# Weighted values summed over a batch's heads in two PSUM banks, batches unrolled

## The reference

```python
q, k, v = (einsum('btm,mhd->bthd', x, w) for w in (w_aq, w_ak, w_av))
q, k = _rope(q), _rope(k)
s = einsum('bihd,bjhd->bhij', q, k) / 128 - 1e30 * (i < j)
p = softmax(s, axis=-1)
o = einsum('bhij,bjhd->bihd', p, v)
r = einsum('bihd,hdm->bim', o, w_ao)        # summed over the heads
x = layernorm(x + r)
h = silu(tlin(x, w1_w, w1_s)) * tlin(x, w2_w, w2_s)
h = gelu(tlin(h, h1_w, h1_s)); h = gelu(tlin(h, h2_w, h2_s))   # erf form
return layernorm(x + tlin(h, w3_w, w3_s))
```

## Time and profile before

| | |
|---|---|
| median of three runs (lowest, highest) | 1098.11 us (1096.88, 1100.96) |
| span of the profiled execution | 1099.5 us |
| instructions | 20887 |
| PE busy, PE weight loads busy | 1008.7 us (92%), 837.4 us (76%) |
| DVE busy | 890.4 us (81%) |
| ACT busy | 657.7 us (60%) |
| POOL busy | 598.5 us (54%) |
| last matmul of attention | about 807.6 us |

### The profile page before, as it was taken

The page is one execution under the profiler, slowest core; times in us unless marked ns, Lnnn a source line. Parts: engine busy times, 40 slices in busy tenths (PEclk is TensorE's granted clock), DMA queues, the critical chain, the costliest instruction groups (busy, mean ns, idle before and its releaser), DMA issues. The chain is left out here.

```text
span 1099.5 us, 20887 instructions
## 1 busy us (share of the span) xinstructions
PE 1008.7 (92%) x5648; PEld 837.4 (76%) x5648; DVE 890.4 (81%) x1803; ACT 657.7 (60%) x1383; POOL 598.5 (54%) x536
## 2 busy tenths in 40 slices
PE   2699999999999999999999999999939999999995
PEld 1588787877878787887878788788727878788784
DVE  4888898989988899998889999898855758576744
ACT  4476776767776676777767777676625252252531
POOL 3667767777777778777777877777540100000000
PEclk8799999999999999999999999999978999999998
DMA  8542222732223242222223122222020000000000
GB/s 281 164 134 49 58 72 63 218 86 57 57 50 74 58 114 86 57 57 61 64 67 105 48 57 58 67 64 60 1 78 1 1 1 20 1 19 0 1 20 19
DMA packets 33838, 69.99 MB, mean 64 GB/s; under 512 B 5520, under 2 KB 7056, under 8 KB 32272
## 3 DMA queue, kind: packets, MB, share of 16 engines
q1 hardware_dynamic: 30976, 62.81, 21.4%
q10 hardware_dynamic: 2832, 6.82, 1.7%
HBM read 24.26 MB, written 7.34 MB: 29 GB/s over the span
## 5 line engine op out<-in xcount | busy, mean ns | idle before, releaser
L737 POOL TENSOR_SCALAR probs<-probs,inv_sum 128x128 f32<-128x128 f32 (+7 forms) x256 | 237.6, 928 | 178.5 <-DVE inv_sum L653 178.5
L554 ACT ACTIVATE pT<-psum 128x512 fp32r<-128x512 f32 (+3 forms) x384 | 176.7, 490 | 146.9 <-PE psum L420 144.7
L310 PE MATMUL psum<-pT,vals 128*128 128x512 f32 (+3 forms) x1152 | 246.9, 355 | 1.6 <-DVE rT L695 1.6
L542 ACT ACTIVATE probs<-psum,neg_max 128x128 f32<-128x128 f32 (+7 forms) x256 | 190.5, 744 | 52.5 <-DVE neg_max L647 49.0
L663 DVE TENSOR_TENSOR pT<-psum,pT 128x512 fp32r<-128x512 f32 (+3 forms) x384 | 199.8, 547 | 15.7 <-ACT pT L554 12.6
L310 PEld LDWEIGHTS psum<-pT,vals 128*128 128x128 f32 x1152 | 191.8, 193 | 24.1 <-DVE pT L663 1.7
L647 DVE TENSOR_REDUCE neg_max<-psum 128x1 f32<-128x128 f32 (+7 forms) x256 | 190.9, 746 | 11.0 <-PE psum L411 10.9
L420 PE MATMUL psum<-ident,probs 128*128 128x128 f32 x1152 | 178.5, 281 | 21.9 <-DVE pT L663 15.4
L742 POOL TENSOR_TENSOR swapped<-swapped,rope 128x512 f32<-128x512 f32 x128 | 165.4, 1292 | 40.5 <-DMA swapped<-proj 40.4
L749 POOL TENSOR_TENSOR qk<-swapped,qk 128x512 fp32r<-128x512 f32 x128 | 179.4, 1402 | 3.6 <-ACT qk L574 3.6
L918 PE MATMUL ps<-hid,w 128*128 128x512 f32 x768 | 181.3, 396 | 0.0
(11 more groups left out here) (78 smaller groups left out, 1241.7 us busy)
## 6 DMA issues: line engine op xcount, KB each, us to landing
swapped<-proj SPq DMA_DIRECT2D x256, 128.0 KB, 2.3
w_stage<-qk_split SPq DMA_DIRECT2D x30, 256.0 KB, 2.7
x_static<-x_moving SPq DMA_DIRECT2D x4, 1024.0 KB, 5.0
wv_stage<-v_split SPq DMA_DIRECT2D x15, 256.0 KB, 2.6
x_split<-ffn_raw ACTq DMA_DIRECT2D x2, 1024.0 KB, 5.9
ffn_raw<-g SPq DMA_DIRECT2D x2, 1024.0 KB, 8.0
x_moving<-x_split SPq DMA_DIRECT2D x2, 1024.0 KB, 4.9
out<-y SPq DMA_DIRECT2D x4, 512.0 KB, 2.6
```

The lines of the kernel that those rows point to most:

```text
L310: ins = nc.tensor.matmul(out_ap, left[a], right[b], start=first and i == 0, stop=last and i == 2)
L542: nc.scalar.activation(probs[:, ib % 4, :width].rearrange("p (h c) -> p h c", h=halves), score_ps[:, ib % 2, :halves, :half], ACT.Exp, bia ...
L554: nc.scalar.activation(pT[chunk][:, 0, 4 * f:4 * f + n_blocks, (ib % 4) * P:(ib % 4 + 1) * P], bank("t", head[1], nth)[:, :n_blocks * P].r ...
L737: nc.gpsimd.tensor_scalar(p, p, inv_sum[:, n:n + 1], 1.0, ALU.mult, ALU.mult).then_inc(probs_ready[0], 1)
```

## The change

The result of `attend` is no longer added head by head. The two halves of the tokens have a bank each (6 and 7), and the matmuls of all eight heads of a batch accumulate there; only the first matmul of the batch's first head overwrites. `take_batch` copies each half to `rT` once per batch, at the steps where the adds stood, and only the first head of the next batch waits for that. The zeroing of `rT` goes. Bank 6 leaves the set that fills, q and k tiles and value tiles share, so that banks 4 and 5 and the lent ones remain; the fourth value tile moves from step 6 to step 7. The loop over pairs 1 to 14 becomes, per batch, one pair written out and a loop over the other three (two in the last batch, whose last pair is written out), so that the batch is known wherever tokens are addressed: value tiles read `x_moving` directly and `x_static` with its four DMAs goes.

```diff
-V_STEP = (4, 5, 6, 6)
+V_STEP = (4, 5, 6, 7)
-ADD0_STEP, ADD1_STEP = 0, 4
+TAKE0_STEP, TAKE1_STEP = 0, 4
-PV_BANK = 7
+PV_BANK = 6
...
-                    uses[use] = [min([4, 5, 6] + lent, key=lambda b: last[b])]
+                    uses[use] = [min([4, 5] + lent, key=lambda b: last[b])]
...
-    pv_ps = psum[:, PV_BANK * BANK:]
+    pv_ps = psum[:, PV_BANK * BANK:].rearrange("p (k c) -> p k c", k=CHUNKS)
...
-            body((-1, 1), s)
-        steps(0, body)
-        with eng.Fori(1, PAIRS - 1) as pair:
-            steps(pair, body)
-        steps(PAIRS - 1, body)
+            body((-1, 1), s, 0)
+        for b in range(B):
+            steps(b, 0, body)
+            with eng.Fori(1, PAIRS_OF - (b == B - 1)) as hp:
+                steps(b, hp, body)
+        steps(B - 1, PAIRS_OF - 1, body)
...
             def stage_x_moving(b):
-                sp.wait_ge(qk_projected[0], NQK * H * (b - 1))
-                sp.wait_ge(x_fixed, 16 * b)
-                sp.dma_start(dst.bitcast(F32), src).then_inc(x_moved, 16)
+                wait_for_pair(sp, v_projected, PAIRS_OF * (b - 1) - 1, NV - 1)
+                sp.dma_start(x_moving[:, b % 2].bitcast(F32), x_split[b - 2]).then_inc(x_moved, 16)
...
-                    if not dynamic:
-                        sp.dma_start(x_static[:].bitcast(F32), x_half.bitcast(F32)).then_inc(x_fixed, 16)
...
-                                          [x_static[:, part, t0:t0 + P] for part in range(2)],
+                                          [x_moving[:, b % 2, part, t0:t0 + P] for part in range(2)],
...
-                    wait_for(pe, pv_added, *earlier(head, chunk, 1, CHUNKS))
+                    if in_batch(head) == 0:
+                        wait_for_pair(pe, pv_taken, number(head) // H - 1, chunk)
...
-                    last = split_products(pv_ps[:, i0:], [vals[:, part, jb, parity(head)] for part in range(2)],
+                    last = split_products(pv_ps[:, chunk, i0:], [vals[:, part, jb, parity(head)] for part in range(2)],
                                           [pT[chunk][:, part, jb, i0:] for part in range(2)],
-                                          jb == 0, jb == 4 * chunk + 3)
+                                          jb == 0 and in_batch(head) == 0,
+                                          jb == 4 * chunk + 3, in_batch(head) != 0)
...
-            def add_head(head, chunk):
+            def take_batch(head, chunk):
-                if not exists(head):
+                if in_batch(head) != H - 1 or not exists(head):
                     return
...
-                wait_for(dve, pv_added, *earlier(head, chunk, 2, CHUNKS))
-                nc.vector.tensor_tensor(acc, pv_ps[:], acc, ALU.add).then_inc(pv_added[0], 1)
+                nc.vector.tensor_copy(rT[:, col:col + BANK], pv_ps[:, chunk]).then_inc(pv_taken[0], 1)
...
-            nc.gpsimd.memset(rT[:], 0.0).then_inc(r_zero, 1)
```

More of the change, by code:

```diff
@@ L246, in run_pairs, with steps, in_batch @@
         for s in range(NI):
-            body((-1, 1), s)
-        steps(0, body)
-        with eng.Fori(1, PAIRS - 1) as pair:
-            steps(pair, body)
-        steps(PAIRS - 1, body)
+            body((-1, 1), s, 0)
[4 more added lines that the diff above has]
+        steps(B - 1, PAIRS_OF - 1, body)
         for s in range(NI):
-            body((PAIRS, 0), s)
-    def steps(pair, body):
+            body((PAIRS, 0), s, B)
+    def steps(b, hp, body):
         for off in range(2):
             for s in range(NI):
-                body((pair, off), s)
+                body((PAIRS_OF * b + hp, off), s, b)
+    def in_batch(head):
+        return number(head) % H if isinstance(head[0], int) else None
     def rope_tasks(head, s, steps):
@@ L304, in wait_for_banks, with split_products @@
                 break
-    def split_products(out_ap, left, right, first, last):
+    def split_products(out_ap, left, right, first, last, onto_earlier=False):
         terms = ((0, 0), (0, 1), (1, 0))
         for i, (a, b) in enumerate(terms):
-            ins = nc.tensor.matmul(out_ap, left[a], right[b], start=first and i == 0, stop=last and i == 2)
+            ins = nc.tensor.matmul(out_ap, left[a], right[b], start=first and i == 0, stop=last and i == 2,
+                                   skip_group_check=onto_earlier)
         return ins
@@ L373, in stage_pair @@
                         stage_for_values()
[L375 to L380, removed]
             stage_pair(0, 0)
             sp.wait_ge(w_saved, W_SAVED)
-            with sp.Fori(1, H // 2) as hp:
+            with sp.Fori(1, PAIRS_OF) as hp:
                 stage_pair(0, hp)
@@ L388, in _ @@
                 sp.dma_start(ffn_raw[:, base:base + src.shape[1]], src).then_inc(ffn_loaded, 16)
-            with sp.Fori(1, B - 1) as b:
-                stage_batch(b)
-            stage_batch(B - 1)
+            for b in range(1, B):
+                stage_pair(b, 0)
+                if b < B - 1:
+                    stage_x_moving(b + 1)
+                with sp.Fori(1, PAIRS_OF) as hp:
+                    stage_pair(b, hp)
         @block.tensor
@@ L490, in step @@
                 for c in v_tasks(head, s):
-                    project_v(head[0], c)
+                    project_v(head[0], b, c)
                 if s in PV0_PIECES and exists(head):
@@ L582, in values_high, with step @@
                                      bank("v", 0, nth), ACT.Copy).then_inc(v_high[0], 1)
-            def step(head, s):
+            def step(head, s, b):
                 ahead = step_on(head, (s + 1) // NI)
@@ L714, in step @@
                     negative_max(step_on(head, (s + 2) // NI), (s + 2) % NI)
-                if s == ADD0_STEP:
-                    add_head(step_on(head, -1), 0)
-                if s == ADD1_STEP:
-                    add_head(step_on(head, -1), 1)
+                if s == TAKE0_STEP:
+                    take_batch(step_on(head, -1), 0)
+                if s == TAKE1_STEP:
+                    take_batch(step_on(head, -1), 1)
                 if exists(head):
```

29 lines of the change are left out of this document (8 added, 21 removed).

## The result

The change makes the kernel slower: 1155.53 us (median of 4 runs, 1151.47 to 1161.36) against 1097.86 us (4 runs on the same chip), a ratio of 1.0525 with a 95% interval of 1.0493 to 1.0558. The prediction was 1169 us, in a range of 1124 to 1194. The profiled execution has a span of 1155.5 us, against 1099.5; a span runs from the first instruction to the last, and the device time of that same execution was 1157.39 us.

What follows compares the result with a forecast made beforehand. PE was taken to bound attention. The profiled 1099.5 us, plus 56 for bank waits, plus 17 for the clock, minus 1.6 at attention's end, gave 1170.9; less 1.4 to the runs' median, rounded to 1169 us, range 1124 to 1194.

Steps and rivals of the forecast that it cites:

- Mechanism and a pair's price: Value tiles wait for banks released by DVE's subtraction of a fill; +3.5 us a pair (2.0 to 4.5), +56 us over 16.
- the bound with DVE free: At v0, were DVE free, copy and subtraction of 4a would still leave a wait of 1.45 us.
- Off 1 unchanged: In off 1 an earlier subtraction gains nothing, since the scores behind it wait for POOL's low part; taken as 0.
- waits of off 1 absorb the stalls: Rival: engines catch up while PE stands in off 0, off 1's 1.5 us go, no clock cost; 1128 us, 15%.
- The path of off 1 gets longer: Rival: v3's later copy makes ACT, then POOL, 0.8 us late in off 1; 13 us on top, 1182 us, 10%.
- Faster: Rival: subtractions run ahead of PE, no bank is late, PE regains 1.8 us a pair and the clock; 1057 us, 6%.
- no change: Rival: banks late in name only, adds were hidden, only 1.6 us at the end of attention seen; 1096 us, 4%.
- Unrolling and token copies at 0: Ends of loop turns and token copies cost PE nothing, so 14 turns becoming 11 and dropping the copies gain 0.
- The clock: PE waits of 2.2 us at v0 were to bring half clock in 13 of 16 pairs; +17 us (0 to +27).
- 10 more at 1.7 us: Clock term: ten additional stretches of half clock on PE, each costing 1.7 us; +17 us.
- some 15: Sign that the forecast is right: some 15 stretches of half clock on PE.
- The end of attention: PE's 1.63 us wait for the add of the last head's first half goes with two result banks; -1.6 us.

Runs made afterwards that it cites:

- the reordered kernel: Changed kernel with DVE subtracting fills before taking the next scores' maximum in steps 4 and 5 of off 0; 1143.31 us, ratio 1.0417.
- The kernel without adds: Kernel before without its 64 adds and PE's waits for them, output wrong, only its time used; 1097.08 us, ratio 0.9994.
- the half version: Changed kernel, but only the second token half accumulates over heads; first half added per head from bank 6, lent in steps 2 to 5; 1097.03 us.
- banks alone: Kernel before with only bank 6 taken from the shared set and the fourth value tile moved to step 7; 1177.07 us, ratio 1.0734.
- after with the low parts on DVE: Changed kernel with the low parts (fp32r remainders) of the first two q or k tiles subtracted on DVE, not POOL; 1142.27 us, ratio 1.0375.

## Why the prediction was right, and where it wasn't

- *Mechanism and a pair's price: right.* v0 2.05 us (forecast 2.2), v1 1.46 (1.2), v2 and v3 0.26 (0.4), less the old 0.32 at 5a. A clean pair (one without a stretch of half clock) grew from 47.38 to 50.93, by 3.55 us, for a forecast of 3.5. The way to get there was to follow DVE's queue up to the subtraction; the bound with DVE free was 1.45, near the 1.30 of the reordered kernel.
- *Off 1 unchanged: right.* 1.5 us before and after. The kernel without adds shows why: only who is waited for changes. The rival "waits of off 1 absorb the stalls" falls, since the rows at 395.53 to 398.17 are there in full. "The path of off 1 gets longer" falls too: POOL's row is 0.85 us where it was 0.69, but the one before it is 0.17 shorter.
- *"Faster" and "no change": fall.* The subtraction of 4a isn't done before v0 in any pair.
- *Unrolling and token copies at 0: right* (1.0004).
- *The clock: wrong, and this is the whole miss.* "10 more at 1.7 us" was the step. Between 48 us and the end of attention before had 6 stretches of half clock and after has 7: five at v0 (from 52.3, 106.9, 158.1, 209.3, 315.1 us), two behind off 1 (345.8, 601.8), and not "some 15". So +1.7 us stands in the place of +17, and the cost that I set on every wait of 2 us comes in few. The price of one was about right: a pair of before with one (224.59 to 273.52) takes 48.93 us, 1.6 more than a clean one. The profiled execution isn't a lucky one: the granted clock of after's four is 0.967 to 0.977 (this one 0.970), and with some 15 stretches it would be near 0.96. On the spans the miss is 1170.9 - 1155.5 = 15.4 us, and the clock is 15.3 of it. On the medians it is 13.5, because I took 1.4 us off the span, while after's median and its profiled span are the same to 0.1 us. Two windows in after, behind waits of 1.96 and 2.05 us at v0 (length, PE, PEld, DVE, ACT, POOL, PEclk, DMA share, GB/s):

```profile
158.10:161.50 3.40, 3.40 (x12) 2.39 (x12) 1.31 (x3) 1.59 (x3) 1.75 (x2) 0.50 0.00 0
...
367.70:371.10 3.40, 3.10 (x19) 2.38 (x19) 1.60 (x4) 2.07 (x4) 2.00 (x3) 1.00 0.00 0
```

The same wait costs the clock in one pair and not in another: 12 matmuls at half clock (1.2 GHz), 19 at full clock (2.4 GHz). I had counted 13 of 16 pairs, because one wait of 1.82 us had been followed by a fall. One case isn't a rate. The Trainium skill, "TensorE: Matmul & The Clock Gate", section "A second HAM failure mode: psum-queue depth-cycling", tells of a clock that goes down and up with small gaps between groups of matmuls, and gives no rate; that every pair would pay was my reading of it. Here 5 pairs of 16 did at v0.
- *The end of attention: half right.* I took off the 1.63 us of the earlier trace rows whole; the row is now

```profile
859.43 4.88 PE L315 MATMUL psum<-pT,vals 128*128 128x512 f32 x24 [0.93 <-DVE pT L653]
```

Directly ahead of the add DVE did the subtraction of the last fill, which PE needs too, so the wait shrank by the add's 0.7 us only.
- *Some pairs* weren't in the sum apart from the others. v0 waits 4.02 us in pair 0 (my bound from the earlier trace rows: 4.2), 2.80 in pair 1, 3.10 in pair 5, and 2.43 to 2.50 in pairs 4, 8 and 12. The last three are the first pairs of a batch: there the copy of the batch before (L681, 0.68 us) stands ahead of the subtraction, where the add stood. Pair 5 shows the reason for 1 and 5, a swap DMA that landed late:

```profile
309.08 1.43 POOL L727 TENSOR_TENSOR swapped<-swapped,rope 128x512 f32<-128x512 f32 x1 [1.10 <-DMA swapped<-proj]
...
310.47 1.27 POOL L734 TENSOR_TENSOR qk<-swapped,qk 128x512 fp32r<-128x512 f32 x1
310.55 1.74 DVE L667 TENSOR_TENSOR swapped<-by_cos,swapped 128x512 f32<-128x512 f32 x1 [1.10 <-POOL swapped L727]
...
312.21 1.08 DVE L637 TENSOR_REDUCE neg_max<-psum 128x1 f32<-128x896 f32 x1
...
313.21 0.87 DVE L653 TENSOR_TENSOR pT<-psum,pT 128x512 fp32r<-128x512 f32 x2
...
313.94 0.98 PE L315 MATMUL psum<-wv_stage,x_moving 128*128 128x256 f32 x6 [3.10 <-DVE pT L653]
```

The missing bank ties PE to everything that stands ahead of the subtraction on DVE, the DMA's landing among it. A third bank doesn't free PE of it altogether: in the kernel with three banks and unrolled batches one such landing made 5a wait 1.50 us in place of 0.3.

```profile
296.16 0.87 PE L409 MATMUL psum<-ident,probs 128*128 128x128 f32 x6 [1.50 <-DVE pT L651]
```

These waits add little to the sum. In pairs 1 and 5 v1 waits 0.4 to 0.5 us less, and pair 0 grew by 2.5 us only: before already stood 1.82 us at its 5a, and the stretch of half clock ahead of attention, 20.5 us long before, is 17.1 us in after. That shorter start gives back some 1.7 us, as much as the seventh stretch costs, and it is chance: other kernels of these experiments have one or the other length.

The sum with what was measured: attention ends at 864.3 us in place of 807.6, so +56.7 (pair 0 +2.5, pairs 1 to 14 +53.2, the last pair and the end +1.0), and the feed-forward part takes 291.2 us in place of 291.9: 1099.5 + 56.7 - 0.7 = 1155.5. (The 0.7 is what the feed-forward part is shorter.) By my own terms, with 56 for the pairs, 1.7 for the clock and 0.7 for the wait at the end of attention, 1099.5 + 56 + 1.7 - 0.7 = 1156.5.

## What to carry to other kernels

A PSUM bank that is held longer is paid for by what shared it: before trading a bank for fewer instructions, find the tightest place of the rotation, and follow the queue of each engine up to the instruction that releases the bank there. Busy time saved on an engine counts only if PE waits for that engine and for nothing else at the same place: 43 us of adds were worth nothing, and 32 of the 64 were worth 0.57 us a pair only after POOL's work had been moved out of the way. A resource may be kept for part of a period: the half version accumulates in one bank, lends the other in the steps that are tight, and loses nothing.

## What the runs showed of the hardware

DVE's sum of two SBUF operands (128x512, fp32) took 1.70 us beside POOL's subtraction and 0.67 without it. The rows of after show how: POOL's L727 ends at 362.47 + 1.29 = 363.76, DVE's L661 beside it at 363.22 + 1.09 = 364.31, 0.55 later; POOL's L734 ends at 365.45, DVE's L667 at 366.01, 0.56 later; in pair 5 POOL ends at 311.74 and DVE at 312.29, again 0.55. From these rows, DVE gets on only when POOL is through. It goes the other way too: POOL's L734, begun at 363.72 while DVE's L661 ran, took 1.73 us, and 1.27 in pair 5, where it began 0.08 us ahead of DVE's. The Trainium skill, "SBUF — State Buffer", section "SBUF: two separate sides", says that a DVE operation with two SBUF inputs and a GpSimd operation that reads SBUF exclude one another for a whole instruction; these rows agree. DVE's L653, one of whose operands is in PSUM, isn't stretched at 366.93 (0.87 us for two, as at 198.33 in the earlier trace rows) beside POOL's L727, which runs from 366.75 to 368.01.

What the clock does behind a gap is a matter of how often. In after, half clock began at waits of 1.92 to 2.05 us at v0 in 2 of 10 pairs, at those of 2.4 to 2.5 us in 0 of 3, at those of 2.8 us and more in 3 of 3. With banks alone it was pair 0 (a wait of 4.02 us) and 8 of the other 15 (2.45 to 2.62 us); in after with the low parts on DVE, 0 of 8 at 1.49 to 1.60 us and 4 of 7 at 1.99 to 2.24. The length of the wait alone doesn't tell which pair pays.
